# Decoder layer: TensorE takes the experts' gate product, and in odd slots the up product, ahead of the product of probabilities and values

## What is computed

```python
# part A, the mixer
x = causal_dwconv(rmsnorm(x)) + x               # 3 taps, then 128 -> 128
x = min_gru(rmsnorm(x)) + x                     # a scan over positions
x = gelu(rmsnorm(x) @ w1 + b1) @ w2 + b2 + x    # 128 -> 512 -> 128
# part B, cross attention: 16 heads of 64, context of 120 positions, causal mask
attn = softmax(q @ k.T / 8 + mask); ctx = attn @ v; out = ctx @ Wo + bo
# part C, 16 experts of width 64, two of them chosen by a router
hg = einsum('bsd,edi->bsei', x, experts_wg); hu = einsum('bsd,edi->bsei', x, experts_wu)
all_outputs = einsum('bsei,eid->bsed', silu(hg) * hu, experts_wd)
out = x + shared_mlp(x) + sum(weight * selected)
```

## Time and profile before

| | before |
|---|---|
| median of 3 runs | 1685.32 us (1680.99 to 1686.09) |
| profiled execution, its own time | 1683.33 us |
| its span, first to last instruction | 1681.5 us |
| mean granted TensorE clock | 0.986 |
| TensorE (PE) busy | 1507.0 us (90%), 11552 matmuls |
| TensorE weight loads (PEld) | 1231.5 us (73%) |
| VectorE (DVE) busy | 1161.7 us (69%) |
| ScalarE (ACT) busy | 866.1 us (52%) |
| GpSimd (POOL) busy | 725.5 us (43%) |

### The profile page before, as it was taken

How to read it: one execution, slowest core, us unless ns; L and a number is a source line. 1 busy time by engine, 2 the same in 40 slices (tenths; PEclk the granted TensorE clock), 3 DMA queues, 4 the chain that set the end, 5 groups by cost and what they waited for, 6 DMA issues and landing times. The chain is left out here.

```text
span 1681.5 us, 32978 instructions
## 1 busy us (share of the span) xinstructions
PE 1507.0 (90%) x11552; PEld 1231.5 (73%) x11552; DVE 1161.7 (69%) x2822; ACT 866.1 (52%) x3177; POOL 725.5 (43%) x882
## 2 busy tenths in 40 slices
PE   2889999989999898998989999998999999899966
PEld 1667777877778777777877777787777778777854
DVE  3566867777676777867677786777768677776732
ACT  3655455454554545555564555546554554655411
POOL 4543535345354534535444453544435453452411
PEclk9999999999999999999999999999999999999977
DMA  3000000000000000000000000000000000000000
GB/s 136 7 7 2 6 15 4 17 3 5 15 4 17 4 16 3 5 15 5 16 3 18 2 6 15 5 16 3 18 1 6 15 5 17 3 6 1 6 2 7
DMA packets 22229, 19.15 MB, mean 11 GB/s; under 512 B 1904, under 2 KB 20912, under 8 KB 22064
## 3 DMA queue, kind: packets, MB, share of 16 engines
q1 hardware_dynamic: 22064, 17.05, 3.2%
HBM read 12.85 MB, written 4.19 MB: 10 GB/s over the span
## 5 line engine op out<-in xcount | busy, mean ns | idle before, releaser
L1247 POOL TENSOR_TENSOR pr<-pr,ri 128x480 f32<-128x480 f32 x256 | 255.5, 999 | 497.7 <-DVE ri L959 497.7
L685 ACT ACTIVATE pr<-sE,nm 128x120 f32<-128x120 f32 x512 | 178.0, 360 | 298.3 <-DVE nm L944 298.1
L422 PE MATMUL pvb<-pT,vv 120*64 120x128 f32 x2048 | 141.8, 281 | 62.5 <-DVE pT L955 60.7
L685 ACT ACTIVATE pr<-sO,nm 128x120 f32<-128x120 f32 x512 | 178.7, 378 | 0.0
L422 PEld LDWEIGHTS pvb<-pT,vv 120*64 120x64 f32 x2048 | 110.6, 138 | 92.6 <-DVE pT L955 83.3
L1266 POOL TENSOR_TENSOR ew<-e,gw 128x512 f32<-128x512 f32 x128 | 134.6, 1052 | 100.8 <-issue 82.3
L955 DVE COPY pT<-t 120x512 f32<-120x512 f32 x256 | 164.1, 682 | 0.0
L390 PEld LDWEIGHTS sE<-kT,qT 64*128 64x128 f32 x1024 | 123.4, 187 | 50.8 <-issue 50.8
L390 PE MATMUL sE<-kT,qT 64*128 64x120 f32 x1024 | 147.0, 284 | 0.0
L390 PE MATMUL sO<-kT,qT 64*128 64x120 f32 x1024 | 147.0, 284 | 0.0
L496 PE MATMUL m<-wd,eT_s 128*128 128x128 f32 x1024 | 137.8, 290 | 2.8 <-ACT eT_s L728 2.8
(11 more groups left out here) (271 smaller groups left out, 3842.1 us busy)
## 6 DMA issues: line engine op xcount, KB each, us to landing
xt<-in_x SPq DMA_DIRECT2D x16, 256.0 KB, 3.0
out_y<-y SPq DMA_DIRECT2D x64, 64.0 KB, 1.5
cT<-in_ctxT SPq DMA_DIRECT2D x16, 240.0 KB, 3.1
hT<-in_w_k SPq DMA_DIRECT2D x1, 512.0 KB, 4.8
qT<-in_w_v SPq DMA_DIRECT2D x1, 512.0 KB, 6.0
qT<-in_w_q SPq DMA_DIRECT2D x1, 512.0 KB, 6.8
wo<-in_w_o SPq DMA_DIRECT2D x1, 512.0 KB, 7.9
qT<-in_w_g SPq DMA_DIRECT2D x1, 512.0 KB, 8.2
```

The costliest lines, as they stand in the source:

```text
L422: ins = mm(pvb[r * DK:(r + 1) * DK, (k // 2) * T:(k // 2 + 1) * T], vv[:, q, h * DK:(h + 1) * DK], pT[:, 4 * r + k // 2, :], start=True, s ...
L685: ins = f(pr[:, p % RING, r, i, :], score_banks[r][:, i * S:(i + 1) * S], ACT.Exp, bias=nm[:, p % 2, r, i:i + 1], accum_out=rsum[:, p % 2, ...
L1247: GP.tensor_tensor(pr[:, p % RING, r, :, :], pr[:, p % RING, r, :, :], ri[:, p % 2, r, :, :].to_broadcast([P, 4, S]), ALU.mult).then_inc(s ...
```

## The change

`c_up` is cut in two: `c_gate` keeps the first half, `c_up` the second. In the slots of TensorE's body both stood together behind `b_pv`, the projections of slots 0 and 1, `c_down` and, in slot 8, `a_norm_T`. Now `c_gate` of every slot, and in odd slots `c_up` behind it, stand ahead of `b_pv`; `c_up` of even slots stays where it was. All waits are kept, each with its product.

```diff
-            def c_up(c, n):
+            def c_gate(c, n):
                 q, half = n // 2, (n % 2) * 512
...
                 product(m0[:], cols_of(x2T, q * T, (q + 1) * T), cols_of(split["wg"], half, half + 512)).then_inc(sem["eg"], 1)
 
+            def c_up(c, n):
+                q, half = n // 2, (n % 2) * 512
                 if n % 2:
                     pe.wait_ge(sem["e_act"], upto("e_act", c, n - 1))
...
                         a_ff1(a, 2)
+                    if C and s < PAIRS:
+                        c_gate(c, s)
+                    if C and odd and s < PAIRS:
+                        c_up(c, s)
                     if B and s >= LAG:
                         b_pv(b, s - LAG)
...
-                    if C and s < PAIRS:
+                    if C and not odd and s < PAIRS:
                         c_up(c, s)
```

## The result

The changed kernel takes 1744.0 us (median of 4 runs, 1743.3 to 1744.58) against 1684.76 us: a ratio of 1.0355, 95% interval 1.0337 to 1.0373. It is slower, as forecast, but by 59 us where the forecast said 38 and the range ended at 1742. The span of the profiled execution grew from 1681.5 to 1741.7 us.

The account below looks back on a forecast made before the run. A ring of dependences across the engines, not TensorE alone, was taken as the bound. Terms of 2.51 us a group, 35.1 in fourteen, made 37.9 us with two other groups: 1723 us, 2.2% slower, range 1702 to 1742.

Parts of the forecast that it names:

- The bound: TensorE looks like the bound at 93% busy, but a ring of dependences across the engines decides.
- the ring through ys, y and ew: Loop actT, scores, pv, down, ys, y, pT, maxima, exponentials, et, ew, actT; its slack in the rows is 0.37 us and 0.
- Slots 0 and 1, +0.84: Gate of slot 0 blocks on sT, delaying projections 20 to 23 and the expert step: 0.84 us more a group.
- Slots 2 to 7, +0.47, +0.78, +0.42: Added us a group: slots 2 and 3 0.47, slots 4 and 5 0.78 (ys 0.91 late in both pairs), slots 6 and 7 0.42.
- ScalarE's tanh comes early, but this saves nothing.: Slots 2 and 3: VectorE and GpSimd steps up to rs stand between ys and y, and y follows rs already.
- priced it at 0.15 us where it stood: Slot 2: by the exclusion rule ssf follows ew (0.76), without it y (0.91): 0.15 us a group, 2 us in all.
- 0.91 ahead of ys: Even slots 2 and 4: gate 0.81 and the switch 0.10 stand ahead of pv and down, so ys comes 0.91 us late.
- The clock: Rival: the wait ahead of gate in slot 0 brings half-clock spells, 1.7 us each, 24 us more, 1747 us; chance 0.07.
- TensorE stays busy some 91%: Argument against the rival in which the new wait ahead of gate in slot 0 lowers the granted clock.
- The group without a mixer: The group without a mixer beside it: expected 2.0 to 3.6 us more, taken as 2.5.
- The last group: Experts alone: the even tanh moves under down but et stays behind ys, 0.1 us in each of three slots.
- The sum: 2.51 us a group, 35.1 in fourteen; with the two other groups 37.9 us, 1723 us, 2.2% slower.

Follow-up runs that it names:

- e2: Kernel before, with gate and up ahead of pv only in odd slots 3, 5 and 7; 1688.04 us, ratio 1.0017.
- e1: Kernel before, with only slots 0 and 1 reordered (gate, and up in slot 1, ahead of projections 20 to 23); 1712.32 us, ratio 1.0159.
- e6: e4 with the wait for sT in slot 0 moved from gate to up; 1688.26 us, ratio 1.0026 to the kernel before the change.
- e7: Kernel before, with only GpSimd's ew of even slots made to wait until y is written; 1663.74 us, ratio 0.9876.
- e10: Changed kernel with the wait for sT in slot 0 moved from gate to up, ew left free; 1720.17 us, ratio 1.0208 to the kernel before.
- e4: Changed kernel, with GpSimd's ew of even slots also waiting until y is written; 1721.58 us, ratio 1.0209 to the kernel before.
- e3: Kernel before, with gate ahead of pv and down only in even slots 2, 4 and 6; 1733.29 us, ratio 1.0281.
- e5: Kernel before, TensorE's order untouched, with two small VectorE reciprocals ahead of y in even slots; 1730.38 us, ratio 1.028.

## Why the prediction was right and wrong

- **The bound.** Right. The waits for pT were filled, 40 us of them, and the kernel got slower: the ring through ys, y and ew decides. e2 shows that the fill of the odd slots alone wins 0.4 us a group in slot 3 and costs 0.75 in slot 7.
- **Slots 0 and 1, +0.84.** Right in size, 0.82 in the changed kernel, 0.78 in e1. It left out what the wait does to the clock.
- **Slots 2 to 7, +0.47, +0.78, +0.42.** The terms of the ring were right as far as they went. e6 and e7 both have ew behind y and no block in slot 0, and differ by the reordering alone. From actT to actT, e6 takes 16.79, 18.17 and 17.74 us, e7 16.22, 17.31 and 17.23: +0.57, +0.86 and +0.51, each about a tenth of a microsecond above its term.
- **"ScalarE's tanh comes early, but this saves nothing."** This is the step that failed. An instruction that becomes ready sooner isn't free: it let ew start between rs and y. The prediction had read this blocking on ssf, cited the rule for it, and priced it at 0.15 us where it stood. It didn't ask where else the order of GpSimd and VectorE would flip. In slot 4 y takes 0.71 us more and gin 0.64 more, and keep, no longer beside ew, takes 0.46 less. So the pT copy of slot 5 comes 5.98 us behind ys instead of 5.09, which is 0.89; with 0.91 ahead of ys that is the 1.80 that was measured, where 0.78 was forecast. In slot 6 y is blocked for 0.71 as well, but only 0.14 of it reaches the next actT (e10 against e6); with the 0.51 of the reordering that is the 0.66 measured, to within 0.01, instead of 0.42. In slot 2 the block moved from ssf (1.01 to 0.16 us) to y (0.35 to 1.06), and that pair cost 0.38. That the forecast of 0.47 came near is partly luck, since it had ssf blocked and y free.
- **The clock.** It was a rival at 0.07, with 1.7 us a spell against 1.57 measured. It came true in part: four groups in the changed kernel, 6 us, and in nine groups of e1 and thirteen of e4. "TensorE stays busy some 91%" was no argument; the mean over a group says nothing of one gap of 2.25 us.
- **The group without a mixer** cost 5.9 us and not 2.5: there slots 0 and 1 cost 1.87, each of the three pairs behind them 1.55, about the 0.91 and the 0.71 of y together, and the rest gave back 0.6.
- **The last group** was put at +0.3 and became 3.6 us shorter (59.49 to 55.90). e3 has this too (55.87), e1 and e2 do not (61.10, 60.62). So it belongs to the early gate of even slots; the prediction missed that gain.
- **The sum.** Between 38 and 60 us lie 22: 1.15 x 14 = 16 from slots 0 to 7, above all from the blocked steps, 6 from the clock, 3.4 from the last attention group, 1.6 in the first bodies, less 3.9 in the last group and 1 in irregular ones. The range took in bounds for each price but no bound for an overlap that turns round, so it ended 2 us short.

What stays open is which groups have a fall of the clock. The same wait of 2.24 or 2.25 us brings it in four, nine or thirteen of fifteen groups, and no run here tells what picks them.

## What to carry to other kernels

Before moving work earlier, follow what its result releases, on every engine, and ask whether it will now start ahead of something that it used to follow. When an instruction's longest duration is three times its median, look at that one instance before the change: its price may be in the trace already. An idle TensorE costs its wait and, now and then, the clock behind it; a wait belongs to the instruction whose bank or tile it guards, not to the first of its group.

## What the runs showed of the hardware

- A VectorE tensor_scalar from SBUF to SBUF (y, ssf, keep, gin) that starts after a GpSimd instruction on SBUF is held until that one ends. On 128 x 128 and 128 x 4 numbers it ends 0.08 and 0.03 us behind it (y 1.06 us instead of 0.35, ssf 1.01 instead of 0.16), on 128 x 512 some 0.3 us behind it (gin 1.33 instead of 0.69). The Trainium skill ("SBUF — State Buffer", Who interferes with whom) has this rule; e4, e5 and e7 agree with it. The two pT copies of slot 3, whose source is PSUM, took their usual 1.28 us in e7 although ew started 0.09 us behind the first and ran beside both.
- The granted clock stayed at 1.00 through an idle stretch of 2.24 us and fell 1.2 us after work began again (767.55 and 768.73 in e4). Filling the idle time with useless matmuls kept it up and saved 18 us.
